# Attention in a fused two-layer kernel: products with V two steps at a time, and twelve slots for finished exponentials

## The reference, cut to what matters

```
scores  = einsum('bhqd,bhkd->bhqk', q, k) * scale
scores  = where(causal, scores, -inf)
weights = softmax(scores, axis=-1)
attn    = einsum('bhqk,bhkd->bhqd', weights, v)
```

## Time and profile before

| | |
|---|---|
| median of 3 timed runs | 3038.05 us (3037.52 to 3038.63) |
| span of the profiled execution, by its records | 3087.2 us |
| attention with exponentials in it, in the trace | 357.2 to 1342.0 us |
| busy in the span: PE, DVE, ACT, POOL | 2657.8, 1991.1, 1684.5, 1217.6 us |
| mean granted TensorE clock | 0.916 |

### The profile page before, as it was taken

One profiled execution on the slowest core, in us unless ns is written; L12 is line 12 of the kernel. 1 busy time (PEld: TensorE's weight loads), 2 busy tenths in 40 slices (PEclk: granted clock), 3 DMA queues, 4 the chain that ended last, 5 costly groups with the idle time before them and its releaser, 6 DMA issues.

```text
span 3087.2 us, 40739 instructions
## 1 busy us (share of the span) xinstructions
PE 2657.8 (86%) x13090; PEld 1344.4 (44%) x13090; DVE 1991.1 (64%) x2854; ACT 1684.5 (55%) x3093; POOL 1217.6 (39%) x1354
## 2 busy tenths in 40 slices
PE   7888889889988898889999997886888888888866
PEld 4555423233232332258888886762222222222222
DVE  7677476777766777001111111653999999999997
ACT  4531366566665666753333332426777677777662
POOL 4330021221112212300000001843988888888885
PEclk9999999999999999899999998997798898897867
DMA  6685313123132230125655654634666666666563
GB/s 210 197 163 162 103 33 57 34 58 51 39 51 45 48 49 18 29 83 184 203 191 189 202 185 154 202 116 102 158 167 160 160 175 163 162 177 157 157 171 96
DMA packets 219923, 390.82 MB, mean 127 GB/s; under 512 B 56777, under 2 KB 156748, under 8 KB 214748
## 3 DMA queue, kind: packets, MB, share of 16 engines
q1 hardware_dynamic: 213596, 371.66, 45.0%
q0 software_dynamic: 6144, 16.82, 1.7%
HBM read 304.61 MB, written 83.79 MB: 126 GB/s over the span
## 4 chain that ended last, share of the span: by engine, by line
PE 52%; DVE 21%; issue 9%; ACT 6%; POOL 4%; DMA 2%; another core or an unknown queue 1%; POOLq 0%; SPq 0%; DVEq 0%; ACTq 0%
PE ps L1749 51%; DVE hh L1722 8%; DVE mp L1526 6%; DVE ps L1709 3%; POOL Ch L950 3%; ACT Pt L1101 1%; DMA dA<-step_rows 1%; ACT dA L1297 1%; PE ps L1950 1%; PE ps L1973 1%; DVE zs L1731 0%; ACT te L1247 0%; ACT te L1250 0%; DVE qr L1443 0%
## 5 line engine op out<-in xcount | busy, mean ns | idle before, releaser
L1526 DVE TENSOR_REDUCE mp<-ps 128x1 f32<-128x1024 f32 (+7 forms) x768 | 667.8, 909 | 216.2 <-PE ps L1749 194.9
L1101 ACT ACTIVATE Pt<-ps 128x512 f32<-128x512 f32 (+3 forms) x1280 | 611.9, 537 | 349.5 <-PE ps L1749 321.4
L1749 PE MATMUL ps<-qk 99*128 99x512 bf16 (+7 forms) x2560 | 628.2, 358 | 91.4 <-DVE mp L1526 51.5
L950 POOL TENSOR_TENSOR Ch<-hh,Cb 128x1024 f32<-128x1024 f32 x256 | 604.6, 2363 | 45.2 <-DVE hh L1722 45.2
L826 POOL TENSOR_SCALAR_AFFINE_SELECT Pt<-Pt 128x128 f32<-128x128 f32 x512 | 146.0, 292 | 868.7 <-ACT Pt L1101 858.4
L1722 DVE TENSOR_TENSOR_SCAN hh<-dA,hst,ps 128x512 f32<-128x512 f32 x384 | 471.5, 1265 | 0.0
L1749 PEld LDWEIGHTS ps<-qk 99*128 99x128 bf16 (+1 forms) x2560 | 208.2, 99 | 538.1 <-DVE mp L1526 204.6
L1297 ACT ACTIVATE dA<-dA,A 128x512 f32<-128x512 f32 x512 | 338.2, 713 | 150.7 <-DMA dA<-step_rows 148.0
L1709 DVE TENSOR_TENSOR ps<-ps,Bb 128x512 f32<-128x512 f32 x512 | 326.3, 683 | 60.6 <-PE ps L1749 59.4
L1577 DVE TENSOR_TENSOR yb<-ps,b2b 128x256 f32<-128x256 f32 x78 | 33.2, 425 | 458.9 <-PE ps L1749 458.9
L1749 PE MATMUL ps<-Pt,vg 128*32 128x512 f32 (+3 forms) x2560 | 312.7, 562 | 2.4 <-POOL Pt L826 2.4
(11 more groups left out here) (289 smaller groups left out, 2965.1 us busy)
## 6 DMA issues: line engine op xcount, KB each, us to landing
dA<-step_rows SPq DMA_DIRECT2D x256, 512.0 KB, 4.7
we<-in_experts SPq DMA_DIRECT2D x39, 2052.0 KB, 7.8
qk<-qk_parts SPq DMA_DIRECT2D x192, 128.0 KB, 5.1
qk_parts<-q SPq DMA_DIRECT2D x32, 384.0 KB, 3.0
expert_out<-yb SPq DMA_DIRECT2D x39, 257.0 KB, 9.4
expert_in<-zero SPq DMA_DIRECT2D x39, 256.0 KB, 5.0
xg<-expert_in SPq DMA_DIRECT2D x39, 256.0 KB, 2.7
step_rows<-dt SPq DMA_DIRECT2D x128, 64.0 KB, 3.6
```

Source lines behind the costliest of these rows:

```text
L950: pool.tensor_tensor(Ch[:, k % 6, :, :], hh[:, k % HRING, :, :], Cb[:, par:par + 1, :].broadcast_to([P, 2, CH]), ALU.mult).then_inc(s_Ch, 1)
L1101: act.activation(Pt[:, n % PRING, q0:CH], ps[:, 4 + n % SRING, q0:CH], ACT.Exp, scale=SCALE).then_inc(s_exp, 1)
L1526: dve.tensor_reduce(mp[:, qc, h, t % TPC, k0 // 1024:k0 // 1024 + 1], slot[:, 0:n], AX.X, ALU.max).then_inc(s_free, 1)
L1749: return pe.matmul(o, lhsT, rhs, start=start, stop=stop, **kw)
```

## The change

The products with V of two steps stand together: steps p and p + 1 behind the last score of step p + 2. `Pt` has twelve slots instead of eight. The counts on `s_pv` start at 3 instead of 2, so that ACT's wait before step s asks for pv s - 3 instead of pv s - 2; the other waits on this semaphore move by the same one and ask for the same pv as before. The PSUM rings (three score banks, two slots for max units) and the places of max, turn and back units in the plan stay as they are.

```diff
-SRING, PRING = 3, 8
+SRING, PRING = 3, 12
...
-        if n % HG == HG - 1 and n > HG:
+        if n % (2 * HG) == HG - 1 and n > HG:
             step = n // HG - 1
-            out.append(("pv", step))
+            out += [("pv", step - 1), ("pv", step)]
...
     if with_exp:
-        out.append(("pv", STEPS - 1))
+        out += [("pv", STEPS - 2), ("pv", STEPS - 1)]
...
-                        sp.wait_ge(s_pv, g * STEPS + KEYS_STEP + 3)
+                        sp.wait_ge(s_pv, g * STEPS + KEYS_STEP + 4)
...
-                    sp.wait_ge(s_pv, (g + 1) * STEPS + 2)
+                    sp.wait_ge(s_pv, (g + 1) * STEPS + 3)
...
-                    pool.wait_ge(s_pv, g * STEPS + 2)
+                    pool.wait_ge(s_pv, g * STEPS + 3)
...
-            pool.wait_ge(s_pv, (NG - 2) * STEPS + 2)
+            pool.wait_ge(s_pv, (NG - 2) * STEPS + 3)
...
-                act.wait_ge(s_pv, g * STEPS + (LAST_STEP[qc] + 1 + 2))
+                act.wait_ge(s_pv, g * STEPS + (LAST_STEP[qc] + 1 + 3))
...
-            pe.sem_inc(s_pv, 2)
+            pe.sem_inc(s_pv, 3)
```

## The result

The changed kernel takes 3079.43 us (median of 4 runs, 3076.73 to 3083.07). The kernel before takes 3037.78 us (median of 4, 3036.23 to 3038.63). The ratio is 1.0139 [1.0124, 1.0153]: slower by 42 us. The forecast was 3081.

A forecast was written before the change was run, and what follows sets the result against it. PE leads, coupled to DVE by a ring of two slots and to ACT by three banks; these rings decide. +39 us for seven full groups and +4 for the last, on 3038, gave 3081 us, range 3060 to 3102.

The forecast's parts named there:

- The pair: Two pv's back to back on PE: 1.90 us, 2.00 with entry, saving 0.18 us per pair against two visits.
- The walk: Max units between pairs, walked: waits 1.14 instead of 0.46 us, +0.50 us per pair, +6 per full group.
- the group's end: Around turn and back and behind the last max unit, four pairs: 0, hidden because PE stands there anyway.
- small units, no waits: First chunk of a full group: two pairs save 0.18 us each, -0.4 us.
- rival 3: More standing in PE calls more stretches at 1.2 GHz; four per full group add 48 us, 3129; chance 0.07.
- The last group: No max units, ACT sets the pace: two steps take 5.28 us against 4.92, +4 us for the group.
- The other edits: Twelve slots and shifted waits on `s_pv`: no time gained by the slots, waits late by one pv at most.
- The sum: +39 us for seven full groups and +4 for the last, on 3038: 3081 us.
- The signs named: Four-step window about 14 us instead of 13.0, PE's row-maxima waits up by half or more, last group about 102 us.
- The first (3010): Waits between PE and DVE do not grow, all 28 us are gained: 3010 us; chance 0.08.
- The second: No change: the extra wait equals what is saved, 3038 us; chance 0.05.
- the fourth: The pair is dearer than two single pv's, over 2.09 us: 3104 us and more; chance 0.05.

The follow-up runs named there:

- e8_no_scatter_single: Kernel before without POOL's indirect DMAs into the experts' input, single pv's: 3036.97 us, ratio 0.9995 to the kernel before.
- e9_no_scatter_pairs: Changed kernel (pairs) without POOL's indirect DMAs into the experts' input: 3082.96 us, ratio 1.0146 to the kernel before.
- e0: Kernel before, unedited, run again on another chip: 3092.86 us.
- e1: Kernel before with twelve slots and shifted `s_pv` counts, old order of pv's: 3087.29 us, ratio 0.9987 to the kernel before.
- e2: Kernel before with twelve slots and pairs in the seven full groups alone: 3129.51 us, ratio 1.0118 to the kernel before.
- e3: Kernel before with twelve slots and pairs in the last group alone: 3092.54 us, ratio 0.9994 to the kernel before.
- e10_placed_but_third: Kernel before with twelve slots, pv's placed where max units would be held, third chunk almost as before: 2994.49 us, ratio 0.9859.
- e11: Kernel before without POOL's indirect DMAs, run once more: 3037.8 us, ratio 1.0 to the kernel before.
- e6: Changed kernel (pairs, twelve slots) with DVE's reductions reading at most 256 columns: 2997.43 us, ratio 0.9693 to the kernel before.

## Why the prediction was right, step by step

**The pair.** 1.86 us from its start to the next matmul (839.53 to 841.39), where 1.90 was taken between 1.83 and 2.09. With 0.10 for the entry a pair costs 1.96 instead of 2 x 1.09, so 0.22 is saved, not 0.18; 152 visits less would be 33 us, if they were all felt. The drain at a change of the tiling mode that the Trainium skill names (TensorEngine Tiling (Array Packing), Key Properties) is paid once a pair: by that rule the trace agrees, and the time still went up.

**The walk.** 7.56 us were walked for the stretch of the earlier trace rows, 7.48 came (7.52 with a pair of 1.86). By chunk, this is what the term was and what the windows of the two orders give. For equal work, the pv of 256 columns (0.57 us) that left the first window is added there and taken off the fourth chunk, and the pv of 512 columns (1.00) that came into the last window is taken off there and added to the steps ahead of it:

| chunk (steps) | predicted | measured |
|---|---|---|
| first (4) | -0.4 | +0.5 (windows -0.1) |
| second (8) | +1.5 | +0.9 |
| third (12) | +2.7 | +1.8 |
| fourth (16), without the group's end | +2.3 | +2.0 (windows +1.6) |
| the group's end | 0 | +1.3 (windows +2.3) |
| one group | +6, taken as 5.6 | +6.5 |
| mean of the seven groups | 5.6 | 6.1 |

The mean is 126.7 us per group after and 120.6 in the order of before. So the term was 39 and measured 43. The total is near because errors cancel: the second, third and fourth chunk were walked too dear by 1.8 us together, and two other steps failed, by 2.2 us together.

The one is the first chunk, "small units, no waits". ACT after, at its start, and in the order of before:

```profile
740.43 4.71 ACT L1101 ACTIVATE Pt<-ps 128x512 f32<-128x512 f32 x12 [1.03 <-PE ps L1749]
```

```profile
597.86 3.60 ACT L1096 ACTIVATE Pt<-ps 128x512 f32<-128x512 f32 x8 [1.03 <-PE ps L1744]
```

Here ACT's exponentials set the pace of the scores. Before, PE did a pv while ACT worked (600.68), and ACT ran dry only behind it; after, twelve exponentials follow each other without a gap, PE goes no faster than they let it, and the pair's whole time comes behind them.

The other is the group's end: I said that what a pair moves there is hidden behind a stall. PE after, at that end:

```profile
858.49 0.27 PE L1946 MATMUL ps<-idf,mn 128*16 128x128 f32 x1 [1.78 <-DVE mn L1531]
858.59 0.85 PE L1749 MATMUL ps<-qk 99*128 99x384 bf16 x3
859.60 0.67 PE L1749 MATMUL ps<-qk 99*128 99x256 bf16 x2 [0.15 <-ACT Pt L1101]
860.20 2.63 PE L1749 MATMUL ps<-Pt,vg 128*32 128x512 f32 x16
```

and in the order of before (`e8_no_scatter_single`):

```profile
710.58 0.27 PE L1941 MATMUL ps<-idf,mn 128*16 128x128 f32 x1 [1.78 <-DVE mn L1526]
710.69 0.33 PE L1744 MATMUL ps<-qk 99*128 99x384 bf16 x1
710.94 1.06 PE L1744 MATMUL ps<-Pt,vg 128*32 128x512 f32 x8
```

Both stand 1.78 us for the transpose of the maxima. From there to the transposes of the output, with the same scores and pv's in between, are 7.39 us after (858.49 to 865.88) and 6.23 before (710.58 to 716.81): +1.16. The clock in this stretch after:

```profile
858.00:859.00 1.00, 0.52 (x3) 0.38 (x4) 0.51 (x3) 0.00 (x0) 0.00 (x0) 0.84 0.00 0
859.00:860.00 1.00, 0.84 (x5) 0.21 (x2) 0.84 (x4) 0.94 (x3) 0.29 (x1) 0.50 0.00 0
```

By these it fell from 2.4 to 1.2 GHz at about 858.7, 0.2 us after the standing ended. This pair, of 512 and 384 columns, takes 2.56 us (860.20 to 862.76); the same pair takes 1.64 at a clock of 1.00 in the first chunk (744.57 to 746.21). So 0.9 of the 1.16 us is the clock. The fall comes in all seven full groups of this trace and of `e9_no_scatter_pairs`, and in two of seven in e8, there 1.5 us after the standing, to windows of 14.8 and 14.9 us. But in the traces of the order of before from slower chips it comes in four or five groups of seven (before, e0, e1), and with pairs in e2 in three. So it needs no pairs, and that they bring it on is not shown; PE also does the same in both orders for 3.5 us ahead of it. Of rival 3 this is what came: one stretch at 1.2 GHz in a group (two in the first), for about 1 us, where the rival had four for 1.7 us each. (Against it stood "waits of 0.6 us" in the third chunk; the earlier trace rows show one of 0.44.)

**The last group.** ACT and PE after, answering to the earlier trace rows:

```profile
1317.64 0.82 PE L1749 MATMUL ps<-qk 99*128 99x512 bf16 x3
...
1321.06 1.92 PE L1749 MATMUL ps<-Pt,vg 128*32 128x512 f32 x16
1322.92 0.82 PE L1749 MATMUL ps<-qk 99*128 99x512 bf16 x3
```

```profile
1318.13 4.03 ACT L1101 ACTIVATE Pt<-ps 128x512 f32<-128x512 f32 x8 [1.25 <-PE ps L1749]
```

Two steps take 5.28 us (1317.64 to 1322.92), the walked number. ACT runs dry for 1.25 us in each pair, where it was 0.39 for each step. In sum e3 gives +5.3 over slots alone, where +4 was taken. The length that I named as a sign, about 102 us, was wrong, since the 98 us that it started from hold two things of their own. From the eviction ahead of it to its own last one the group takes 96.0 us after, at a clock of 1.00, and 92.3 us in `e10_placed_but_third`, whose last group has the order of before and a clock of 1.00 too: +3.7 at equal clock. In e8 and e11, of the order of before as well, the clock falls early in this group, to 0.94 and 0.96 on the mean, and it takes 95.5 and 95.0 us; so on a chip of 3038 us only 0.5 to 1.0 is left between the orders. And in the 98 us of the earlier trace rows four steps take 14.4 us, where they take 9.8 in e8:

```profile
1299.40:1313.80 14.40, 9.84 (x54) 2.59 (x52) 0.68 (x2) 8.86 (x17) 7.88 (x10) 0.91 0.32 101
```

```profile
1310.36 1.08 ACT L1101 ACTIVATE Pt<-ps 128x512 f32<-128x512 f32 x2 [3.24 <-remote]
```

That is the stall at the start of the fourth chunk, in the last group too.

**The other edits.** Taken at 0. e1 shows -5.6 us on a chip of 3093 us; on one of 3038 us it was not measured. The trace can't part an ACT wait on `s_pv` from one on a score, as PE releases both; but slots and counts alone cost nothing (e1).

**The sum.** 39 + 4 became 43 from the groups and 0.5 to 5 from the last one: 44 to 48 by the traces, 42 by the timed runs of the change, 40 to 46 in all comparisons of the two orders. That the groups' term is off by 4 us and not more is partly luck, as the table shows. It also was right, again partly by luck, to set the difference on the timed 3038 and not on the profiled span: the terms came from stretches that last the same on both chips, and none from the one with the stall.

**The signs named.** Pair and next score: as said. A four-step window of about 14 us: the one in the place of 825.20 to 838.20 takes 13.40 (824.20:837.60) against 13.00, less than said, and the next one 13.80 against 12.90. PE's waits up by half or more: missed for weight loads (24.9 to 28.1), met only for what stands under PE itself (3.8 to 10.2); together 9.6 us, a third. The walk's own 0.63 us for each of the 14 pairs that it gave a longer wait makes 8.8 us; the sign was set higher than my own numbers bore out.

**The rivals.** The first (3010) falls: the extra wait was 0.43 us plus what a pair saved in the stretch above, where less than 0.18 was needed. It would hold with DVE's reductions short, and e6 shows that even then ACT's ring takes most of it back. The second and the fourth fall with the ratio and the 1.86 us; of the third one fall in a group came, as said above.

## What to carry to other kernels

In an order that one engine works off in sequence, work of another kind between two uses of a short ring is the ring's cover: before gathering such work to save a fixed cost per visit (here 0.22 us), walk the ring with both sides' durations and price the wait that is laid bare (here 0.65 us). The same walk shows where a piece of cover is worth most: moved singly to the places where a slot is held, the same products made the kernel 1.4% faster instead of 1.4% slower. When two orders are compared window by window, count the work in each window first: here a single pv that moved across a border was worth 1.00 us, nearly as much as what was looked for. And compare traces only after their executions' own times have been laid beside the timed runs: chips differ by more than the change.

## What the runs showed of the hardware that was not expected

- The same kernel on one core takes 3038 us on one chip and 3090 and 3093 us on two others. The profile of before has waits there whose releaser it can't name, over 480 to 1240 us:

```profile
ACT Pt L1101 <- remote: 12.5, 8, 4.0
...
DVE mp L1526 <- remote: 7.2, 3, 3.2
```

  They lie at the start of the fourth chunk, in all eight groups; the trace after and e8 have none of them. Attention lasts 984.2 us in the profile of before and 937.3 in e8, so 47 of the 49 us lie there. The cause stays open.
- Every full group of the kernels with full reductions, other than e10, has one standing of 1.78 us, for the transpose of the maxima, amid otherwise dense work. The granted clock fell to its lower level 0.1 to 0.4 us behind it in all seven groups of the trace after (a pair then took 2.56 us instead of 1.64), 1.5 us behind it in two of seven in e8, and around it in four or five of seven in the traces of before, e0 and e1. In e10, where the same standing is 0.8 us, the clock stayed at 1.00 in every full group from the second on. Waits of 0.3 us amid full-width work left it at 1.00 in every window shown. The Trainium skill (TensorE: Matmul & The Clock Gate, "A second HAM failure mode") tells of short idling between groups of matmuls that makes the clock swing; the waits of 0.3 us here did not.
- A second product in the same tiling mode, back to back, costs 0.86 us (1.86 - 1.00), where one by itself costs 1.09 with its entry: that is the 0.85 us which the prediction took for its streaming.
